# Graph attention's edge pass with destination rows in two float32r parts, three gathered tiles of four added by TensorE, and edge products issued four at a time

## What is computed

```python
for k in range(Wl.shape[0]):                 # 3 layers
    xl = x @ Wl[k] + bl[k]
    xr = x @ Wr[k] + br[k]
    ef = ea2 @ We[k]                         # 2 numbers for each edge -> 512
    m = leaky_relu(xl[src2] + xr[dst2] + ef, 0.2)
    logit = m @ att[k]
    alpha = _segment_softmax(logit, dst2, n)
    out = segment_sum(xl[src2] * alpha[:, None], dst2, num_segments=n) + b_out[k]
    h = out + x                              # then layer norm, gain, relu
```

## Time and profile before

| | |
|---|---|
| Time, median of 3 runs | 2105.02 us (2102.8, 2105.02, 2105.4) |
| Span of the profiled execution | 2104.3 us |
| The three layers of graph attention, 579 to 1190 us of it | 611 us |
| The three edge passes in them | 98.1 us each, 294.3 us |
| TensorE busy over the span | 92% |
| VectorE busy over the span | 46% |
| Granted clock of TensorE, mean of the span | 0.968 |

### The profile page before, as it was taken

How to read it: one execution, slowest core, us unless ns; L and a number is a source line. 1 busy time by engine, 2 the same in 40 slices (tenths; PEclk the granted TensorE clock), 3 DMA queues, 4 the chain that set the end, 5 groups by cost and what they waited for, 6 DMA issues and landing times. The chain is left out here.

```text
span 2104.3 us, 27610 instructions
## 1 busy us (share of the span) xinstructions
PE 1939.0 (92%) x9070; PEld 1014.7 (48%) x9115; DVE 972.1 (46%) x2915; ACT 441.4 (21%) x1150; POOL 319.1 (15%) x342
## 2 busy tenths in 40 slices
PE   8998988999889899989998699879789999979998
PEld 4454546777543333333433233334434444457876
DVE  7463454000269987998899711156421111041002
ACT  0162441111170061025004212136110000010000
POOL 0000000333227303720570000000000000010001
PEclk9999999999999899989999999989899999999999
DMA  4003019998248405720677199952460220079874
GB/s 160 1 1 101 0 52 359 402 334 314 58 148 245 120 1 189 207 74 1 176 211 256 42 332 386 345 174 69 149 220 1 85 85 0 0 259 404 338 295 165
DMA packets 179978, 355.51 MB, mean 169 GB/s; under 512 B 28640, under 2 KB 38129, under 8 KB 179837
## 3 DMA queue, kind: packets, MB, share of 16 engines
q1 hardware_dynamic: 156860, 283.43, 37.4%
q0 software_dynamic: 22976, 70.23, 11.4%
HBM read 331.94 MB, written 21.67 MB: 168 GB/s over the span
## 5 line engine op out<-in xcount | busy, mean ns | idle before, releaser
L1098 PEld LDWEIGHTS ps<-tokT,w 128*128 128x128 f32 x2304 | 259.8, 192 | 10.7 <-issue 6.7
L1098 PE MATMUL ps<-tokT,w 128*128 128x128 f32 x2304 | 260.6, 275 | 3.1 <-DVE tokT L1243 3.1
L1544 POOL DMA_INDIRECT w<-xl_d,src_i x216 | 213.6, 989 | 319.9 <-DMA xl_d<-XL 249.7
L1660 PE MATMUL ps<-w,oht 128*128 (+1 forms) x660 | 180.7, 381 | 3.8 <-issue 3.8
L1321 POOL DMA_INDIRECT spread_d<-N,slot x12 | 11.8, 979 | 697.8 <-DVE slot L1202 694.8
L1660 PEld LDWEIGHTS ps<-w,oht 128*128 128x128 bf16 x684 | 57.5, 98 | 117.9 <-issue 89.8
L1117 PE MATMUL ps<-w,O 128*128 128x512 f32 x256 | 111.2, 592 | 0.0
L1665 PE MATMUL ps<-w,ident 128*128 128x512 f32 x216 | 110.3, 592 | 0.0
L1257 DVE TENSOR_TENSOR hT<-act,ps 128x512 f32<-128x512 f32 x20 | 13.7, 687 | 177.2 <-ACT act L1150 177.2
L1902 DVE SCALAR_TENSOR_TENSOR w<-ps,w 128x512 f32<-128x512 f32 x114 | 78.6, 690 | 5.7 <-PE ps L1665 0.9
L1692 PE MATMUL ps<-w 128*128 128x512 f16 x304 | 73.7, 398 | 7.4 <-DVE w L1981 7.4
(11 more groups left out here) (507 smaller groups left out, 3049.7 us busy)
## 6 DMA issues: line engine op xcount, KB each, us to landing
w<-L_ffn_W SPq DMA_DIRECT2D x16, 2048.0 KB, 12.9
w<-L_ffn_W SPq DMA_DIRECT2D x8, 4096.0 KB, 17.2
w<-fc1T SPq DMA_DIRECT2D x32, 1024.0 KB, 14.2
w<-fc2T SPq DMA_DIRECT2D x32, 1024.0 KB, 14.3
w<-L_ffn_w_gate SPq DMA_DIRECT2D x20, 1024.0 KB, 9.1
w<-L_ffn_w_up SPq DMA_DIRECT2D x20, 1024.0 KB, 11.8
w<-L_ffn_w_down SPq DMA_DIRECT2D x10, 2048.0 KB, 14.1
w<-L_ffn_w SPq DMA_DIRECT2D x8, 2048.0 KB, 13.4
```

Source lines behind the costliest of these rows:

```text
L1098: m = pe.matmul(k.ps[:, 1 + (q * ins + i) % 4, s * P:(s + 1) * P], self.W1[u][i][:, f, (q * T + s) * P:(q * T + s + 1) * P], self.tokT[:, ...
L1544: gp.indirect_dma_start(self.G[:, u, :], None, k.xl_d, bass.IndirectOffsetOnAxis(ap=k.src_i[:, i:i + 1].bitcast(U32), axis=0)).then_inc(k. ...
L1660: m = pe.matmul(bank, self.oht[:, i * P:(i + 1) * P], self.XP[:, q].rearrange("p t n -> p (t n)")[:, bass.ds(at, D)], start=False, stop=(q ...
```

## The change

- The one-hot matrix of a tile is first copied by ScalarE from bf16 to float32r (`self.wide`, eight slots of 128 x 128), one copy per tile and layer, 228 in all. A new semaphore `widened` tells TensorE. ScalarE may write slot i % 8 when the product of tile i - 8 is done; in layers 2 and 3 it also waits, once, for the end of the aggregation before. In the first layer the copies alternate with the tiles of `pen`.
- xr is held in two float32r parts, not three bf16 ones. VectorE makes them with two instructions for each tile, not four, and TensorE makes two products for each edge tile, not three.
- TensorE adds the gathered rows of three tiles of four, not of two. VectorE adds only those of tiles with i % 4 = 3 (`by_vector`).
- TensorE issues the edge parts of four tiles, not of two, before the rest of these four.
- `r` has four slots, not eight.

The core of the diff:

```diff
-        self.XP = room[:, 0:3072].bitcast(BF16).rearrange("p (q t n) -> p q t n", q=3, t=T)
-        self.r = [room[:, 3072 + u * D:3072 + (u + 1) * D] for u in range(DEEP)]
+        self.XP = nc.alloc_sbuf_tensor_at(f"XP_{k.uid}", [P, 2, T, D], F32R, offset=ahead.room_at)[:]
+        self.wide = nc.alloc_sbuf_tensor_at(f"wide_{k.uid}", [P, DEEP, P], F32R, offset=ahead.room_at + 4 * 6144)[:]
+        self.r = [room[:, 4096 + u * D:4096 + (u + 1) * D] for u in range(QUAD)]
...
-        for two in range(0, EA, 2):
-            for i in (two, two + 1):
+        for quad in range(0, EA, QUAD):
+            for i in range(quad, quad + QUAD):
                 if i >= DEEP:
-                    if i % 2:
-                        pe.wait_ge(self.summed.sem, self.summed.at(EA // 2 * l + (i - DEEP) // 2 + 1))
+                    if self.by_vector(i):
+                        pe.wait_ge(self.summed.sem, self.summed.at(self.QUADS * l + (i - DEEP) // QUAD + 1))
...
-                for q in range(3):
-                    m = pe.matmul(bank, self.oht[:, i * P:(i + 1) * P],
+                pe.wait_ge(self.widened.sem, self.widened.at(EA * l + i + 1))
+                for q in range(2):
+                    m = pe.matmul(bank, self.wide[:, i % DEEP, :],
                                   self.XP[:, q].rearrange("p t n -> p (t n)")[:, bass.ds(at, D)],
-                                  start=False, stop=(q == 2 and i % 2 == 1))
-                if i % 2 == 0:
+                                  start=False, stop=(q == 1 and self.by_vector(i)))
+                if not self.by_vector(i):
                     self.landed(pe, l, i)
                     m = pe.matmul(bank, k.ident[:], self.source(i), start=False, stop=True)
                 m.then_inc(self.product.sem, 1)
...
+    def by_vector(self, i):
+        return i % QUAD == QUAD - 1
...
-            for i in range(EA if l == 0 else 0):
-                a.activation(self.pen[:, i * P:(i + 1) * P], k.ramp[:, 0:P], ACT.Square, scale=FAR,
-                             bias=self.dst_far[:, i:i + 1]).then_inc(self.pens.sem, 1)
+            if l:
+                a.wait_ge(self.aggregated.sem, self.aggregated.at(T * l))
+            for i in range(EA):
+                if i >= DEEP:
+                    a.wait_ge(self.product.sem, self.product.at(EA * l + i - DEEP + 1))
+                a.activation(self.wide[:, i % DEEP, :], self.oht[:, i * P:(i + 1) * P], ACT.Copy
+                             ).then_inc(self.widened.sem, 1)
+                if l == 0:
+                    a.activation(self.pen[:, i * P:(i + 1) * P], k.ramp[:, 0:P], ACT.Square, scale=FAR,
+                                 bias=self.dst_far[:, i:i + 1]).then_inc(self.pens.sem, 1)
...
             ch.link(v.tensor_copy(parts[0], bank))
-            ch.link(v.tensor_tensor(rest, bank, parts[0], ALU.subtract))
-            ch.link(v.tensor_copy(parts[1], rest))
-            v.tensor_tensor(parts[2], rest, parts[1], ALU.subtract).then_inc(self.xr_parts.sem, 1)
+            v.tensor_tensor(parts[1], bank, parts[0], ALU.subtract).then_inc(self.xr_parts.sem, 1)
```

More of the change, by code:

```diff
@@ L22 @@
 U32 = mybir.dt.uint32
+F32R = mybir.dt.float32r
 ALU = mybir.AluOpType
@@ L1417, in __init__ @@
          self.rows_ready, self.xr_parts, self.product, self.summed, self.dotted, self.linear, self.logit,
-         self.low, self.rows_copied, self.pens, self.low_turned, self.low_parts, self.looked_up, self.shifted, self.exped, self.halves,
+         self.low, self.widened, self.rows_copied, self.pens, self.low_turned, self.low_parts, self.looked_up, self.shifted, self.exped, self.halves,
          self.chosen, self.high, self.added, self.tile_out, self.tile_turned, self.tile_cols, self.aggregated) = signals(
@@ L1421, in __init__ @@
              "stats", "root", "normed", "gat_turned", "gat_cols", "xl_done", "xr_done", "rows_ready", "xr_parts",
-             "product", "summed", "dotted", "linear", "logit", "low", "rows_copied", "pens", "low_turned", "low_parts",
+             "product", "summed", "dotted", "linear", "logit", "low", "widened", "rows_copied", "pens", "low_turned", "low_parts",
              "looked_up", "shifted", "gat_exped", "halves", "chosen", "high", "added", "tile_out", "tile_turned",
@@ L1881, in source_rows @@
         for t in range(T):
-            rest, bank, parts = self.xr[:, t % 2, :], k.ps[:, t, :], [self.XP[:, q, t, :] for q in range(3)]
+            bank, parts = k.ps[:, t, :], [self.XP[:, q, t, :] for q in range(2)]
             v.wait_ge(self.xr_done.sem, self.xr_done.at(T * l + t + 1))
             ch.link(v.tensor_copy(parts[0], bank))
-            ch.link(v.tensor_tensor(rest, bank, parts[0], ALU.subtract))
-            ch.link(v.tensor_copy(parts[1], rest))
-            v.tensor_tensor(parts[2], rest, parts[1], ALU.subtract).then_inc(self.xr_parts.sem, 1)
+            v.tensor_tensor(parts[1], bank, parts[0], ALU.subtract).then_inc(self.xr_parts.sem, 1)
             if t < T - 1:
@@ L1892, in edge_logits @@
     def edge_logits(self, v, l, words):
-        k, H = self.k, EA // 2
+        k = self.k
         def dot(i):
-            if i % 2:
-                v.wait_ge(self.summed.sem, self.summed.at(H * l + i // 2 + 1))
-                rows = self.r[i % DEEP]
+            if self.by_vector(i):
+                v.wait_ge(self.summed.sem, self.summed.at(self.QUADS * l + i // QUAD + 1))
+                rows = self.r[i % QUAD]
             else:
@@ L1901, in dot @@
                 rows = k.ps[:, (i + T) % DEEP, :]
-            v.scalar_tensor_tensor(self.r[i % DEEP], rows, 0.0, self.att8, ALU.max, ALU.mult,
+            v.scalar_tensor_tensor(self.r[i % QUAD], rows, 0.0, self.att8, ALU.max, ALU.mult,
                                    accum_out=self.sdot[:, i:i + 1]).then_inc(self.dotted.sem, 1)
@@ L1928, in edge_logits @@
         for i in range(EA):
-            if i % 2:
+            if self.by_vector(i):
                 v.wait_ge(self.product.sem, self.product.at(EA * l + i + 1))
                 self.landed(v, l, i)
-                v.tensor_tensor(self.r[i % DEEP], k.ps[:, (i + T) % DEEP, :], self.source(i), ALU.add
+                v.tensor_tensor(self.r[i % QUAD], k.ps[:, (i + T) % DEEP, :], self.source(i), ALU.add
                                 ).then_inc(self.summed.sem, 1)
@@ L2052, in gat @@
                                     g.tile_turned, g.tile_cols, g.aggregated)],
-             *[(x, EA * L) for x in (g.product, g.dotted, g.low, g.chosen, g.high, g.added)],
-             (g.summed, EA // 2 * L))
+             *[(x, EA * L) for x in (g.product, g.dotted, g.low, g.widened, g.chosen, g.high, g.added)],
+             (g.summed, Q * L))
         done((k.pool_step, 1), (k.counted, 2), (k.ranked, 1), (k.scattered, 16 * ET), (k.sorted, 16),
@@ L2083, in __init__ @@
         self.room = room[:]
+        self.room_at = k.nc.sbuf_top
         self.W1 = [room[:, u * T * self.FF:(u + 1) * T * self.FF].rearrange("p (f n) -> p f n", f=T) for u in range(2)]
```

1 line of the change is left out of this document (added).

## The result

| | before | changed kernel |
|---|---|---|
| Median of the timed runs | 2104.8 us (2102.8 to 2105.4) | 2096.4 us (2094.4 to 2101.4) |
| Ratio, 95% interval | | 0.9963 (0.9948 to 0.9978) |
| Repeated with more runs | 2106.1 us | 2094.8 us; 0.9945 (0.9932 to 0.9958) |
| Span of the profiled execution | 2104.3 us | 2099.5 us |

The gain is 8.4 us in the first comparison and 11.3 in the repeat. The forecast was 22.7 us. The time lies inside the range (2077 to 2100), but well outside the forecast's own band (2077 to 2091).

A forecast was written before the change was run, and what follows sets the result against it. TensorE was taken to bound the edge passes, VectorE 5% behind. Three passes gain 23.9 us, less 1.1 for loads and 0.1 for gathers: -22.7 us, from 2105.0 to 2082.3 us; range 2077 to 2100 (80%).

The forecast's parts named there:

- the forecast's own band: Span of 2077 to 2091 us around the forecast time, given a chance of 74%.
- edit 1's 0.43 us: Edge parts by four on TensorE: one group in place of two, worth 0.43 us in four tiles.
- the row x2: TensorE's timeline row of two edge parts, 0.39 us long: read as running side by side, the group costing 0.43 us.
- both dear rivals: TensorE's float32r products: half-speed stream, 0.43 us each, 2178 us, 12%; or float32's full price, 2375 us, 3%.
- the gathers are just in time: GpSimd's gathers: lead used up just at the first layer's end; 0.1 us of wait taken, 3 as upper bound.
- the forecast's 4.73: TensorE's need in us for four tiles of an edge pass after the change, 0.43 less than 5.16.
- edit 2's price: Two float32r products for three bf16 ones, at 0.215 us each: TensorE gets back 0.86 us in four tiles.
- the 0.43 of the rival: Float32r streams at half speed on TensorE, 0.43 us a product: 73.5 us lost, 2178 us; chance 12%.
- The bare load behind the group: Float32r weight load after TensorE's edge group: at most 0.09 us more, 57 times; taken at 0.02 each, 1.1 us.
- edit 3: TensorE adds three gathered tiles of four: +0.86 us for TensorE, -0.60 for VectorE, keeping VectorE from bounding at 4.88.
- a cheaper group: TensorE's edge group costing a little less than 0.43 us, allowed for by the range's low end, 2077 us.
- the rival of the gathers: GpSimd sets the pace, gathers slowing to 1.37 us; a pass gains 2 to 5 us: 2091 to 2099; chance 5%.

The follow-up runs named there:

- the kernel with edit 1 alone: The kernel before with only the edge parts issued by four; xr in three bf16 parts, TensorE adds two of four: 2092.8 us, ratio 0.9939.

## Why the prediction was right and wrong

**Right**: that TensorE's issue sets the pace and VectorE stands 5% behind; edit 1's 0.43 us and its reading from the row x2 (0.40 us for x4); that float32r is one load and one stream, so both dear rivals fell; that ScalarE's copies and the end of the pass cost nothing; that the gathers are just in time: the changed kernel is slower than the forecast's 4.73 and so does not test it, but the kernel with edit 1 alone runs at 4.74 without a wait of TensorE for a landing in the first pass. VectorE's need was read well: 4.88 forecast, 4.87 in the mean when it took over. In the changed kernel its holes are (94.12 - 82.89) / 19 = 0.59 us in four tiles where 0.45 stood, since the period is longer.

**The step that failed is edit 2's price.** Two terms were too small:

- A float32r product at 0.215 us, measured 0.23. It was worked out by counting streams, and no row showed it. The two bounds that I gave, 0.215 and 0.86, had the one at the foot of the range as the value taken, and no price between 0.215 and the 0.43 of the rival was weighed. Eight of them: 0.12 us in four tiles, 57 x 0.12 = 6.8 us.
- The bare load behind the group: bounded about rightly ("at most 0.09 us more, 57 times"), but taken at 0.02 since "the 0.43 us of the present group already holds a load". It holds a load of 98 ns; the added 91 ns came on top in full, 0.10. This is 57 x 0.08 = 4.6 us over the 1.1 that I took.

Together the two took 0.22 us of the 0.43, and 11 of the 22.7 us. Without float32r (5.60 against 4.95 us) the same 0.65 for edit 2 comes out, and not 0.86. The rule of the Trainium skill that I set beside this edit ("TensorE: Matmul & The Clock Gate", weight-path perf modes: the fast weight load is off for FP32) spoke of this term and in this direction; the trace agrees (189 against 98 ns), and where no stream covers it, behind the group, the difference is paid. The Trainium skill's "FP8 and Floating Point Precision", under TensorE precision notes, gives a 4-byte reduced-precision read without a speed; the runs show 0.23 us for 512 columns.

**A judgement that hung on it.** I wrote that edit 3 "is what keeps VectorE from becoming the bound at 4.88". With TensorE at 4.73 that was so. With TensorE at 4.95 the third tile costs more than it saves: the run with two of four ends the second pass after 96.4 us, that with three after 99.0. That TensorE (4.73) would stand 10% above VectorE (4.28) was in my own sum. A split between the two was there to be asked for, though at the measured prices it proved no better than leaving edit 3 out.

That the time lies inside the range is luck. Its low end, a cheaper group, had no ground; its high end took in the result only through the rival of the gathers, whose mechanism did not come.

## What to carry to other kernels

Where a change gives and takes nearly equal amounts on the bound engine (here -0.86 and +0.86 us, with 0.43 left), a price that is 7% off on eight instructions and a load that lies bare at one place and grows by 91 ns can eat half of the net. So price first the operations that no row shows, and put the forecast between their bounds and not at the cheap end. And when a kernel moves work from one engine to another, write both needs per period side by side and ask for the ratio that makes them equal: here 4.52 against 4.58 us was worth 18 to 21 us where 4.95 against 4.28 was worth 8 to 11. Then measure the simpler split too, and look for a third limit. Leaving the work where it was (4.09 against 4.87) was worth 18 us, which these times do not tell from the balanced split, and with either split the gathers hold up the first pass.

## What the runs showed of the hardware

- Four products of 15 rows in four strips of the array cost as much as two: 0.43 us for the group, 0.40 us from the first start to the last end.
- float32r: one load of 189 ns and one stream, 0.23 us for 512 columns at the full clock and 0.12 for 256; bf16 takes 0.215, float32 0.86. Loads of 189 ns are not seen between streams, at most 0.004 us each between those of 0.12 us, but the 91 ns that a load grew are seen in full behind a group of edge parts (0.10 us, and 0.05 less with a load 53 ns shorter).
- Where the granted clock fell in the stages between the passes changed from kernel to kernel (0.90 to 0.92 in one stretch with the same work), and with it some us of a single execution.
